# A one-layer token tower: more shared groups moved ahead of the experts, fed from stored turned rows

## The reference, cut to what matters

```python
table = where(is_num[:, None], sin(num_value[:, None] / 1000 * freqs), weight)   # 12500 x 128
h = table[x]                                             # 128 x 128 tokens
# attention: 8 heads of 64
q, k, v = heads(layernorm(h) @ Wq), heads(layernorm(h) @ Wkv)
dots = q @ k.T * scale[head];  dots[i == j] = -1e-9
dots = mix over heads with mix_pre;  p = softmax(dots)
p = mix over heads with mix_post;    h = h + (p @ v) @ Wout + bout
# feed-forward: D=128 -> FF=512 -> 128, gelu exact
x2 = layernorm(h).reshape(16384, 128)
y = gelu(x2 @ Ws1 + bs1) @ Ws2 + bs2                     # shared
for bank in ("sp", "fq"):                                # two banks of 8 experts
    probs = softmax(x2 @ Wr + br); expert = argmax; gate = max
    pos = rank of the token among those of its expert; keep = pos < 1280
    y += gate * keep * expert_mlp[expert](x2)            # 128 -> 512 -> 128
return h + y
```

## Time and profile before

| | before |
|---|---|
| time, median of 3 runs | 1506.09 us (1505.55 to 1506.47) |
| time of the profiled execution | 1516.0 us |
| span of the profiled execution | 1514.3 us |
| mean granted TensorE clock | 0.997 of full |
| TensorE matmuls busy | 1465.3 us (97%) |
| TensorE weight loads busy | 1339.9 us (88%) |
| VectorE busy | 1047.0 us (69%) |
| ScalarE busy | 1146.8 us (76%) |
| GpSimd busy | 959.1 us (63%) |

### The profile page before, as it was taken

The page is one execution under the profiler, slowest core; times in us unless marked ns, Lnnn a source line. Parts: engine busy times, 40 slices in busy tenths (PEclk is TensorE's granted clock), DMA queues, the critical chain, the costliest instruction groups (busy, mean ns, idle before and its releaser), DMA issues. The chain is left out here.

```text
span 1514.3 us, 33889 instructions
## 1 busy us (share of the span) xinstructions
PE 1465.3 (97%) x11160; PEld 1339.9 (88%) x11160; DVE 1047.0 (69%) x2811; ACT 1146.8 (76%) x3477; POOL 959.1 (63%) x991
## 2 busy tenths in 40 slices
PE   5789999999999999999999999988999999999999
PEld 2469888888888988889888898877999999999999
DVE  7887788788777887778887787763344333356665
ACT  5589888888888888888888888865555555555555
POOL 7175567888788888788878877664677566510000
PEclk9999999999999999999999999999999999999999
DMA  7324511211211111111111111022244234456665
GB/s 237 132 73 163 164 38 49 69 48 42 60 38 39 55 42 36 35 56 34 36 56 34 37 38 48 26 60 67 69 116 106 70 71 109 120 158 190 189 184 146
DMA packets 171503, 126.48 MB, mean 84 GB/s; under 512 B 30309, under 2 KB 154959, under 8 KB 171330
## 3 DMA queue, kind: packets, MB, share of 16 engines
q1 hardware_dynamic: 153794, 104.15, 23.3%
q0 software_dynamic: 17536, 20.17, 4.8%
HBM read 61.64 MB, written 78.66 MB: 93 GB/s over the span
## 5 line engine op out<-in xcount | busy, mean ns | idle before, releaser
L1129 ACT ACTIVATE expd<-masked,nmax 128x128 f32<-128x128 f32 x1024 | 396.0, 393 | 0.3 <-DVE nmax L1282 0.3
L925 POOL TENSOR_TENSOR prob<-expd,rtotal 128x1024 f32<-128x1024 f32 x128 | 243.5, 1902 | 117.3 <-DVE rtotal L1251 115.8
L1265 DVE COPY_PREDICATED masked<-off_diag,ps_s 128x1024 f32<-128x1024 int32 x128 | 175.0, 1367 | 164.3 <-PE ps_s L1018 164.3
L1062 PE MATMUL ps_o<-u,probT 128*128 128x128 f32 x2048 | 249.0, 275 | 0.0
L1062 PEld LDWEIGHTS ps_o<-u,probT 128*128 128x128 f32 x2048 | 238.9, 191 | 0.0
L1129 ACT ACTIVATION_READ_ACCUMULATOR expd<-masked,nmax 128x1 f32 x1024 | 197.0, 192 | 0.0
L1138 ACT ACTIVATE u<-ps_ut 128x1024 f32<-128x1024 f32 x128 | 131.4, 1026 | 66.3 <-PE ps_ut L1073 66.3
L1227 DVE TENSOR_TENSOR w_lo<-ps_w,w_hi 128x512 fp32r<-128x512 f32 x256 | 164.3, 681 | 0.9 <-ACT w_hi L1167 0.9
L1167 ACT ACTIVATE w_hi<-ps_w 128x512 fp32r<-128x512 f32 x256 | 146.1, 595 | 15.7 <-PE ps_w L1048 9.3
L1158 ACT ACTIVATE probT<-ps_ut 128x1024 f32<-128x1024 f32 x128 | 131.4, 1027 | 33.9 <-PE ps_ut L1030 27.5
L1046 PE MATMUL ps_w<-xT_hi,M_hi 128*128 128x256 f32 x512 | 154.1, 301 | 3.0 <-DVE xT_lo L1221 2.2
(11 more groups left out here) (261 smaller groups left out, 3824.9 us busy)
## 6 DMA issues: line engine op xcount, KB each, us to landing
turned<-x2T SPq DMA_DIRECT2D x32, 256.0 KB, 2.2
answers_sp<-zeros SPq DMA_DIRECT2D x16, 512.0 KB, 4.3
answers_fq<-zeros SPq DMA_DIRECT2D x16, 512.0 KB, 3.8
xT<-turned SPq DMA_DIRECT2D x56, 128.0 KB, 2.3
sh_back<-answers_sp SPq DMA_DIRECT2D x56, 128.0 KB, 2.4
sh_back<-answers_fq SPq DMA_DIRECT2D x56, 128.0 KB, 2.5
out<-res SPq DMA_DIRECT2D x56, 128.0 KB, 2.1
h_sb<-in_L_tok_weight SPq DMA_DIRECT2D x12, 512.0 KB, 5.9
```

The source lines that it names most:

```text
L925: nc.gpsimd.tensor_tensor(prob[k % 2][:, :].rearrange("p (g j) -> p g j", g=H), expd[k % 2][:, :].rearrange("p (g j) -> p g j", g=H), rtot ...
L1062: mm = nc.tensor.matmul(ps_o[:, 0:D], probT[k % 2][:, g * N:(g + 1) * N], u[k % 2][:, g * D:(g + 1) * D], start=(g == 0), stop=(g == H - 1))
L1129: ins = nc.scalar.activation(expd[(k - 1) % 2][:, g * N:(g + 1) * N], masked[(k - 1) % 2][:, g * N:(g + 1) * N], ACT.Exp, bias=nmax[(k - 1 ...
L1265: nc.vector.copy_predicated(masked[k % 2][:, :].rearrange("p (g j) -> p g j", g=H), off_diag[:, :].unsqueeze(1).to_broadcast([P, H, N]), p ...
```

## The change

`HEAD` becomes 20: the head stage takes 20 groups of 256 tokens and the shared stage 44. A head group's turned rows are no longer made anew but loaded by SP from `turned` (`load_head`) into four places (`head_x`); `head_norm`, its transposes and `norm2` go. The up-products take turns between `ps_s` and the pair `ps_w` (`up`). The three tables change. GpSimd sends both banks' rows of the 16 late tiles after its loop (`late_sends`), each send behind a given head group's up or down, and the block ends only when all have landed; the experts' late sends go. In the shared stage the head tokens' sums are made for 256 rows at every second step from 1, the first bank's at step k and the second's at k + 1, with the first bank's ahead of the group's own sums of the next step.

In the setup: `kept` is stored sooner and holds the plain numbers (converted, not divided), so that VectorE divides the gathered own numbers itself, after chunk 5's reduction; the halves are made by two instructions instead of four; the turn constants (six small instructions) and both prefills go to GpSimd, the prefills behind its mixing; its gathers of own numbers stand ahead of its fills and gathers of own rows; the products and turns on TensorE start a chunk later; `WARM` becomes 6.

```diff
-HEAD = 8
+HEAD = 20
-WARM = 13
+WARM = 6
...
+            link.inc(nc.gpsimd.tensor_scalar(turn_b, row_f[:, :], TURN_HI, 0.0, ALU.mult, ALU.add))
...
+            def own_row(t):
                 nc.gpsimd.indirect_dma_start(h_sb[:, (VS + t) * D:(VS + t + 1) * D], None, weight,
                                              bass.IndirectOffsetOnAxis(ap=ids0[:, t:t + 1], axis=0)).then_inc(S["rows0"], 16)
 
+            pool.wait_ge(S["ids0"], 16)
+            pool.wait_ge(S["kept"], 32)
+            for t in range(OWN):
+                own_number(t)
...
-            for c in range(2 * HC):
-                mix(c)
...
+            for t in range(2):
+                own_row(t)
...
+            for t in range(2, OWN):
+                own_row(t)
+            pool.wait_ge(S["coef_out"], 2)
+            pool.wait_ge(S["wT_out"], 1)
+            for c in range(2 * HC):
+                mix(c)
+            for k in range(2):
+                link.inc(nc.gpsimd.tensor_copy(masked[k][:, :].rearrange("p (g j) -> p g j", g=H),
+                                               diag[:, :].unsqueeze(2).to_broadcast([P, H, N])))
...
+            sp.wait_ge(S["numbers"], 2)
+            sp.dma_start(kept[0:P * VR, :].rearrange("(p r) c -> p (r c)", p=P),
+                         numbers[:, 0:VR, :].rearrange("p r c -> p (r c)")).then_inc(S["kept"], 16)
...
+                for n in {6: (0,), 7: (1,), 8: (2,), 9: (3,), 10: (4,), 11: (5,), 12: (6, 7)}.get(c, ()):
                     for half in range(2):
-                        product((c - 5) // HC, (c - 5) % HC, half)
+                        product(n // HC, n % HC, half)
...
+            def thousandths(at, flags=False):
+
+                value, (q, hi, lo) = numbers[:, at, 0], (part[:, n, at] for n in range(3))
...
+                if flags:
+                    dve.wait_ge(S["isn"], 32)
+                    nc.vector.tensor_copy(numbers[:, 0:VR, 1].bitcast(I32), isn[:, 0:VR]).then_inc(S["numbers"], 1)
+                    nc.vector.tensor_copy(numbers[:, VR:VS, 1].bitcast(I32), rest_isn[:, 0:1]).then_inc(S["numbers"], 1)
...
+                high, low = (num_hl[:, chunks, 0:n, k:PARTS:2] for k in range(2))
+                both = src.unsqueeze(3).to_broadcast([P, chunks.stop - chunks.start, n, 2])
+                link(nc.vector.tensor_copy(high, both))
+                nc.vector.tensor_tensor(low, both, high.bitcast(F32), ALU.subtract).then_inc(S["num_f"], 1)
...
+            link(nc.vector.tensor_copy(numbers[:, 0:VS, 0], num_i[:, :]))
+            thousandths(slice(0, VS), flags=True)
+            halves(slice(0, CHUNKS - 1), VC)
...
+                    thousandths(slice(VS, VX))
...
+        AFTER = {129: (1,), 130: (2,), 131: (3,), 132: (4,), 135: (5,), 136: (6,), 137: (7,), 139: range(8, HEAD + 2)}
+        BEHIND = {128: (0,), 129: (1,), 130: (2,), 131: (3,), 132: (4,), 135: (5,), 137: (6,), 139: range(7, HEAD + 2)}
+        BESIDE = {128: (0,), 129: (1,), 130: (2,), 131: (3,), 132: (4,), 135: (5,), 136: (6,), 137: (7,), 139: range(8, HEAD + 2)}
...
+        SENDS_FROM = HEAD - 2 - (TILES - LATE)
...
+        def up(m, f):
+
+            return hidden(ps_s, f) if m % 2 == 0 else ps_w[f // 2][:, f % 2 * GROUP:(f % 2 + 1) * GROUP]
+
+        def head_x(n):
+
+            return expd[0][:, n % 4 * GROUP:(n % 4 + 1) * GROUP] if n % 4 > 1 else x1[n % 4][:, :]
...
+            def load_head(groups):
+                for n in groups:
+                    need(sp, S["head_xlo"], n - 3)
+                    sp.dma_start(head_x(n), turned[n // 2, :, n % 2 * GROUP:(n % 2 + 1) * GROUP]).then_inc(s_head[n % 4], 16)
...
+                    for k in range(2):
+                        sp.wait_ge(s_kept[k], 16 * (HEAD // 4 + 1))
+                    sp.wait_ge(S["x_turned"], GROUPS)
+                    load_head(range(2))
+                    sp.wait_ge(S["normed"], TILES - 1)
+                    load_head(range(2, 4))
+                if q == QUADS - 2:
+                    load_head(range(4, 8))
+            load_head(range(8, HEAD))
...
+            def late_sends():
+                for n in range((TILES - LATE) * BANKS):
+                    q, b, e = n // BATCH // BANKS, n // BATCH % BANKS, n % BATCH
+                    t = LATE + q * BATCH + e
+                    if e == 0:
+                        pool.wait_ge(S["routed"], t // BATCH + 1)
+                    if n % 2 == 0:
+                        pool.wait_ge(S["head_up"], n // 2 + SENDS_FROM)
+                    else:
+                        pool.wait_ge(S["head_down"], n // 2 + SENDS_FROM - 1)
+                    send(nc, sent, x2, to_row, t, b, s_sent[t // 2 % 8])
...
-                    if n < HEAD:
-                        pe.wait_ge(S["head_made"], n + 1)
-                        need(pe, S["head_xlo"], n - 1)
-                        need(pe, S["w_lo"], GROUPS * 4)
-                        for b in range(2):
-                            mm = nc.tensor.transpose(ps_w[n % 2][:, b * P:(b + 1) * P], x1[n % 2][:, b * D:(b + 1) * D], ident[:, :])
-                        mm.then_inc(S["head_turned"], 1)
...
-                        need(pe, S["head_gelu"], m)
+                        pe.wait_ge(S["w_lo"], GROUPS * 4)
+                        need(pe, S["head_gelu"], m - 1)
                         for f in range(FC):
-                            h = hidden(ps_s, f)
+                            h = up(m, f)
...
-                        act.wait_ge(S["head_turned"], n + 1)
+                        act.wait_ge(s_head[n % 4], (n // 4 + 1) * 16)
...
-                if isinstance(i, int) and k in LATE_AT:
-                    send(nc, sent, x2, to_row, LATE + LATE_AT.index(k), 1, S["late"])
...
+        HEADS_FROM = 1
+
+        def head_group(k):
+
+            n = (k - HEADS_FROM) // 2
+            return n if (k - HEADS_FROM) % 2 == 0 and 0 <= n < HEAD else None
...
+                n = head_group(k)
+                if n is not None:
                     dve.wait_ge(s_one[n % 2], (n // 2 + 1) * 32)
+                    need(dve, S["one_out"], n)
+                    for b in range(2):
+                        t = 2 * n + b
+                        ins = nc.vector.scalar_tensor_tensor(one_part[:, b, :], one_back[0][n % 2][:, b, :], gates[:, 2 * t:2 * t + 1],
+                                                             h_sb[:, t * D:(t + 1) * D], ALU.mult, ALU.add)
+                    ins.then_inc(S["one_part"], 1)
+                n = head_group(k - 1)
+                if n is not None:
+                    dve.wait_ge(S["one_part"], n + 1)
                     need(dve, s_one_put[n % 2], n // 2 * 16)
-                    need(dve, S["one_out"], n)
-                    nc.vector.scalar_tensor_tensor(one_part[:, :], one_back[0][n % 2][:, :], gates[:, bass.ds(t * 2, 1)],
-                                                   h_sb[:, bass.ds(t * D, D)], ALU.mult, ALU.add).then_inc(S["one_part"], 1)
-                    dve.wait_ge(S["one_part"], n + 1)
-                    nc.vector.scalar_tensor_tensor(one_out[n % 2][:, :], one_back[1][n % 2][:, :], gates[:, bass.ds(t * 2 + 1, 1)],
-                                                   one_part[:, :], ALU.mult, ALU.add).then_inc(S["one_out"], 1)
```

More of the change, by code:

```diff
@@ L331, in setup @@
         ps_c = pb("ps_c", 512)
-        names = ("made", "num", "isn", "ids0", "numbers", "kept", "small", "freq", "numbers0", "rows0", "stat0", "early_put", "num_f", "numT", "numT_out", "angle", "whole", "reduced", "turn", "sine", "done", "put",
+        names = ("made", "num", "isn", "ids0", "numbers", "kept", "small", "freq", "numbers0", "rows0", "stat0", "early_put", "num_f", "numT", "numT_out", "angle", "whole", "reduced", "turn", "link", "sine", "done", "put",
                  "weights", "wT", "wT_out", "coef", "coefd", "coef_out", "mixed", "M", "hi")
@@ L608, in _ @@
             angles(1)
-            pe.wait_ge(S["num_f"], 2)
             for c in range(4, CHUNKS - 1):
@@ L631, in _ @@
         def _(dve):
[L632 to L636, removed]
+            link = Chain(dve, S["link"])
+            def thousandths(at, flags=False):
+                value, (q, hi, lo) = numbers[:, at, 0], (part[:, n, at] for n in range(3))
                 link(nc.vector.tensor_scalar(q, value, 0.001, None, ALU.mult))
@@ L651, in halves @@
[L651 to L654 removed]
+                src = part[:, 0, chunks.start * VC:chunks.start * VC + (chunks.stop - chunks.start) * n].rearrange("p (c r) -> p c r", r=n)
+                high, low = (num_hl[:, chunks, 0:n, k:PARTS:2] for k in range(2))
+                both = src.unsqueeze(3).to_broadcast([P, chunks.stop - chunks.start, n, 2])
@@ L668, in _ @@
-            halves(slice(0, 4), VC)
-            thousandths(slice(4 * VC, VS))
-            halves(slice(4, CHUNKS - 1), VC)
-            dve.wait_ge(S["isn"], 32)
-            link.inc(nc.vector.tensor_copy(numbers[:, 0:VR, 1].bitcast(I32), isn[:, 0:VR]))
-            link.wait()
```

(11 more changed lines are left out.)

136 lines of the change are left out of this document (46 added, 90 removed).

## The result

| | before | after |
|---|---|---|
| time, median of 4 runs | 1505.82 us (1504.11 to 1506.47) | 1529.60 us (1527.33 to 1533.16) |
| ratio after / before | | 1.0162, 95% interval 1.0139 to 1.0185 |
| profiled execution, span | 1514.3 us, of an execution of 1516.0 | 1525.6 us, of an execution of 1527.3 |
| first attention matmul | 64.85 | 70.91 |
| experts' first transposes | 1052.89 | 1102.62 |

The change made the kernel 24 us slower; 1505.7 was forecast. The two profiles are only 11.3 us apart, so about half of the loss isn't in their difference. Timeline of the kernel after: of the setup; TensorE in the head stage, a late pair of head groups, the first matmuls of the experts and of the shared stage.

A forecast was written before the change was run, and what follows sets the result against it. TensorE was taken as the bound, with time won or lost only where it waits. Setup +3.0, head stage -4.0 and shared stage +0.65 summed to -0.35: 1505.7 us, range 1500.0 to 1511.5.

The forecast's parts named there:

- I carry every difference over to the median unchanged: Whole kernel: differences priced against the profiled execution, 9.9 us over the median of 1506.09, apply to the median unchanged.
- The setup, +3.0: Setup: the changed chain to the halves, one more product and fewer warming matmuls cost +3.0 us, bounds +0.7 and +7.3.
- Rival 1: Slower: mixing starts just before VectorE's copy in the setup and holds VectorE; setup +7.3, total 1510 us; chance 0.22.
- Step (a): Setup: own numbers come sooner, so GpSimd's mixing starts between 22 and 26 us, against 23.9 now.
- Step (b): Setup: GpSimd copies two prefills behind its mixing, 1.05 us each, and they hold VectorE: +2.1 us.
- Step (c): Setup: VectorE's eight dependent steps for thousandths of four columns, behind the hold, at 0.2 us each: +1.6 us.
- (d): Setup: eight products instead of seven follow the halves on TensorE: +2.0 us.
- (e): Setup: with 6 warming matmuls the sine ends the stage: -0.6 us.
- The head stage, -4.0: Head stage: lost transposes and 5.65 us of waits against some 7.0 save 4.0 us, between -2 and -6.
- rival 4: Slower: SP cannot keep up in the shared stage, +6 us, total 1511 us; chance 0.04.
- Rival 2: Faster: TensorE, fuller ahead of the experts, keeps its clock at their start, -3.4 us, total 1502.3 us; chance 0.15.
- rival 3: Faster: GpSimd ready with `diag`, its copies hold nobody, setup +0.7; head stage gives 5; total 1502.5 us; chance 0.16.

## Why the prediction was wrong

**The base.** The step that failed first is "I carry every difference over to the median unchanged". The text itself said that the profiled execution was 9.9 us over the median, and the setup's hold was its largest wait; the second profile of before shows that both were the same 10 us (the setup 9.8 shorter, the span 10.4). By their times most executions have no hold, so a change that brings it in every profiled execution loses these 10 us besides what the two first profiles show. Had the gap been looked for in the trace, the hold was TensorE's longest wait (10.66; the next was 8.0, at its first matmul).

The rest shows in the first two profiles: the experts' first transposes came 49.7 us later, not 37, for 38.0 moved, 6.1 of the setup instead of 3.0, and 5.6 in between instead of -4.0.

**The setup, +3.0.** It measured +6.1. Rival 1 had the mechanism (GpSimd wins by a little, the prefills lengthen the hold, the steps come behind it) and put the halves at 47.9; they came at 47.55. Its total of 1510 was wrong by the base and by the head stage. Step (a) failed: the mixing began at 26.05, the end of the range, and VectorE did not have "the copy and the next reduction (2.8 us) done", since that copy began only at 26.10. Step (b) was right: the prefills took 2.01 (2.1 taken) and VectorE's hold ran through them. Step (c), +1.6, was right behind a hold (45.28 to 47.11), and wrong by a factor of nine in turns with GpSimd (1.82 a step). From the halves to the attention it took 23.4 us against 22.75, so (d) and (e) made +0.6 together, not +1.4.

On the hold, the Trainium skill, "SBUF — State Buffer", section "Who interferes with whom", says that whoever issues first has the shared ports for the whole instruction. The traces show more: the hold lasted over eight products and two prefills that followed without a pause (17.93 us), and over memsets between them in another run (18.27). It ended at a pause of 0.08 us, or else with the second prefill: there VectorE was done at 44.03, 1.15 behind the prefills' end, though an IOTA had followed at once (42.85). Held for one instruction alone, VectorE would have waited at most the 1.9 us of a product.

**The head stage, -4.0.** The step that failed is the walk: "together 5.65" of idle time. Measured: 1.21, 2.31, 2.67, 0.40, 1.54, 0.40 and 2.55, 11.1 in all. The 2.31 was foreseen (2.4). The last u was put 1.05 late and came 2.67 late. The wait for x2 (1.54) was not in the walk. The low part of group 7, which the table puts behind the last batch's routing on VectorE, was not in it either (2.55). And the clock, taken as unchanged, fell twice (3.4). The sum itself holds once the tables of before stand, with the waits for the one up place gone: -4.8 against the -4.0 of the forecast. Moved groups were not quite free: 3.22 each, where 3.17 was taken, is 0.6 for the twelve, and just over the 3.2 that the prediction named as a sign against it.

**The rest.** The first pair of sums in the shared stage delays the low part once, as foreseen, by 0.88 in one profile and 1.42 in the other instead of 0.65; after that TensorE waits for neither sums nor loads, so rival 4 fell. Rival 2's condition came true and was worth little. The two pauses at the experts' start were the same (0.85 and 0.78), but the clock stayed at 1.00 in both profiles of the kernel after (0.66 and 0.83 over ten us in those of before). In the first of these TensorE then waited 1.18 for rows instead of 0.61 and 0.37, and the experts' stage gained 2.2 against the first profile of before and 0.5 against the second. Why the clock stayed was not tried. Of rival 3 neither part came: the setup and the head stage both cost more. Two sums are off by a little, and nothing hangs on them: rival 1's halves at 47.9 are 5.8 late, not 5.9, and rival 4's total is 1511.7, not 1511.

## What to carry to other kernels

If the profiled execution is longer than the median, find the difference in its trace before pricing a change: it may be an event that other executions don't have, and that the change makes certain or takes away. Small dependent VectorE steps beside a long run of GpSimd instructions can cost a GpSimd product each (1.82 us here), once the engines take turns. Leaving the steps out gave 11 us back; moving them ahead of that run would be the way to keep them, and was not tried. An interleaving written by hand for one set of waits is to be walked anew on every engine, and kept where it is not shown to lose; here the old tables with the new head path, and the old setup, make the fastest version (1500.67).

## What was not expected of the hardware

One start decides for a whole run. Where the first VectorE copy to meet GpSimd's products began while GpSimd was inside an instruction, VectorE was out until the products, and the prefills where they stood behind them, had ended, 15.58 to 18.52 us, or until a pause of 0.08 us. It was so 0.05 to 0.44 us into a product, and also beside a memset or a gather with the products right behind, though the copy was then 0.54 or 0.55 us ahead of the first product. Where the copy began while GpSimd was idle, waiting 0.29 to 0.35 us for another engine, GpSimd's first product waited and both took turns from then on, for 16 to 20 us. A gather alone holds nothing: beside one from 20.38 the kernel after ran a copy in 1.28 us. Why turns, once taken, go on, and what exactly decides at the start, was not tried.
